# Rotary queries and keys of a decoder layer: the PSUM copy on ScalarE, the shuffle from SBUF, the cosine product on GpSimd

## What is computed

```python
qkv = layernorm(x) @ w_atten.T
q, k, v = split(qkv, 3)                      # 16 heads of 32 features
x0, x1 = even, odd features of q (and of k)
rotated = [x0 * cos - x1 * sin, x1 * cos + x0 * sin]
att = softmax(causal(rotated_q @ rotated_k.T / sqrt(32)))
x = x + (att @ v) @ w_proj.T
x = x + cross_attention(layernorm(x), ctx)
x = x + moe(layernorm(x))
```

## Time and profile before

| | |
|---|---|
| median of 3 runs | 1183.74 us (1178.89 to 1186.48) |
| profiled execution | 1181.09 us, its span 1179.3 us |
| PE busy | 1069.3 us, 91% |
| DVE busy | 600.1 us, 51% |
| ACT busy | 490.7 us, 42% |
| POOL busy | 177.7 us, 15% |

### The profile page before, as it was taken

How to read it: one execution, slowest core, us unless ns; L and a number is a source line. 1 busy time by engine, 2 the same in 40 slices (tenths; PEclk the granted TensorE clock), 3 DMA queues, 4 the chain that set the end, 5 groups by cost and what they waited for, 6 DMA issues and landing times.

```text
span 1179.3 us, 18650 instructions
## 1 busy us (share of the span) xinstructions
PE 1069.3 (91%) x6128; PEld 762.2 (65%) x6128; DVE 600.1 (51%) x1592; ACT 490.7 (42%) x1269; POOL 177.7 (15%) x204
## 2 busy tenths in 40 slices
PE   5778899799988898998988899998999999999998
PEld 2344444445544455445464678987889888889997
DVE  3456626656546666365464545563443344443565
ACT  1246634446615556345475432313443344342221
POOL 2121102211101112021100000011211111111232
PEclk9879999799999899998999999998999999999999
DMA  5934503213503335033160301135244444422554
GB/s 180 223 55 60 66 17 54 43 25 62 89 2 54 55 54 108 1 54 54 22 160 1 110 27 63 36 112 205 90 149 158 145 145 145 153 82 89 169 163 152
DMA packets 55524, 107.14 MB, mean 91 GB/s; under 512 B 5584, under 2 KB 16336, under 8 KB 55440
## 3 DMA queue, kind: packets, MB, share of 16 engines
q1 hardware_dynamic: 49840, 87.72, 31.5%
q0 software_dynamic: 5600, 18.35, 5.5%
HBM read 59.66 MB, written 21.23 MB: 69 GB/s over the span
## 4 chain that ended last, share of the span: by engine, by line
PE 73%; DVE 13%; issue 5%; DMA 4%; ACT 4%; POOL 1%; DVEq 0%; SPq 0%; ACTq 0%; POOLq 0%
PE ps L1005 19%; PE ps L812 10%; PE ps L1015 10%; PE ps L835 5%; PE ps L863 5%; PE ps L904 4%; PE ps L854 4%; PE ps L926 3%; PE ps L824 2%; PE ps L995 2%; DMA ks<-rope_b 2%; DVE gu_lo L1277 2%; DVE probs L1161 2%; DMA routed_x<-xn_d,table_cur 2%; PE ps L1023 1%
## 5 line engine op out<-in xcount | busy, mean ns | idle before, releaser
L1161 DVE CUSTOM_DVE_ANT_0 probs<-ps,mask 128x128 f32<-128x128 f32 (+3 forms) x256 | 123.8, 489 | 189.1 <-PE ps L824 129.4
L631 ACT COPY probsT<-ps 128x128 f32<-128x128 f32 (+3 forms) x256 | 109.3, 427 | 186.6 <-PE ps L835 185.5
L824 PE MATMUL ps<-ks,qs 96*128 96x256 f32 (+2 forms) x256 | 143.0, 562 | 26.5 <-DVE mx L1161 19.9
L623 ACT ACTIVATE probs<-probs,nb 128x128 f32<-128x128 f32 (+3 forms) x256 | 145.9, 570 | 49.3 <-DVE nb L1166 48.7
L812 PE MATMUL ps<-xnT,wa_sb 128*128 128x512 f32 x256 | 126.7, 620 | 16.0 <-DVEq L1147 15.2
L835 PE MATMUL ps<-ident,probs 128*128 128x128 f32 x640 | 125.0, 297 | 0.3
L1416 DVE TENSOR_TENSOR hidden<-sg,ps 128x352 f32<-128x352 f32 x69 | 35.9, 520 | 151.5 <-ACT sg L719 151.5
L835 PEld LDWEIGHTS ps<-ident,probs 128*128 128x128 f32 x640 | 81.2, 149 | 45.7 <-issue 39.2
L719 ACT ACTIVATE sg<-ps 128x352 f32<-128x352 f32 x69 | 32.0, 464 | 182.9 <-PE ps L1005 179.6
L824 PEld LDWEIGHTS ps<-ks,qs 96*128 96x128 f32 x256 | 52.3, 204 | 63.4 <-issue 35.7
L1015 PE MATMUL ps<-d_hi,h_hi 128*128 128x512 f32 (+1 forms) x207 | 89.9, 434 | 1.3 <-DVE h_lo L1420 1.3
(11 more groups left out here) (155 smaller groups left out, 1988.8 us busy)
## 6 DMA issues: line engine op xcount, KB each, us to landing
gu_raw<-in_we SPq DMA_DIRECT2D x10, 1408.0 KB
y_d<-y_sb SPq DMA_DIRECT2D x37, 256.0 KB
qs<-rope_b SPq DMA_DIRECT2D x32, 256.0 KB, 5.0
ks<-rope_b SPq DMA_DIRECT2D x32, 256.0 KB, 6.2
shared_x<-xn_d SPq DMA_DIRECT2D x32, 256.0 KB
d_raw<-in_we SPq DMA_DIRECT2D x10, 512.0 KB
qs<-rope_a SPq DMA_DIRECT2D x16, 256.0 KB, 7.0
ks<-rope_a SPq DMA_DIRECT2D x16, 256.0 KB, 6.6
```

The lines of the kernel that those rows point to most:

```text
L623: nc.scalar.activation(pr, pr, ACT.Exp, bias=nb[:, n % 2, h:h + 1], scale=SCALE, accum_out=sums[:, n % 2, h:h + 1]).then_inc(exp_done, 1)
L631: nc.scalar.copy(probsT[n % 2][:, h, 0:w], ps[:, T_BANK + h % 2, 0:w]).then_inc(pT_done, 1)
L824: nc.tensor.matmul(ps[:, S_BANK + h % 2, 0:w], qs[:, g % 2, h, i * P:(i + 1) * P], ks[:, g % 2, h, 0:w], start=True, stop=True).then_inc(s ...
L1161: nc.vector.tensor_tensor_reduce(probs[n % TT][:, h, 0:w], ps[:, S_BANK + h % 2, 0:w], mask[:, TOKENS - w:], 1.0, LOWEST, ALU.add, ALU.max ...
```

## The change

ACT copies the raw queries or keys from `QK_BANK` to `rope_b` (`copy_raw`), right behind its `probsT` copy of the same place, or behind the exponentials where there is none, and the end of this copy releases the bank (`rope_copied` replaces `qk_used`). DVE's shuffle reads this copy in SBUF. The cosine product goes to GpSimd, in place on `rope_b` and behind the sine product. DVE's add waits for both products. The add, the rounding copy, the subtraction, the tables of places and the DMAs stay.

```diff
--- before.py
+++ after.py
@@ -295,9 +295,10 @@
         v_mm = sem("v_mm")
         v_done = sem("v_done")
         qk_mm = sem("qk_mm")
-        qk_used = sem("qk_used")
         rope_link = sem("rope_link")
+        rope_copied = sem("rope_copied")
         rope_sine = sem("rope_sine")
+        rope_cosine = sem("rope_cosine")
         rope_done = sem("rope_done")
         stacked = sem("stacked")
         s_mm = sem("s_mm")
@@ -362,7 +363,7 @@
         W_LOADS = 7
         STACK = 2 * 3 * 16
         ROUTER_LINKS = 19
-        ROPE_LINKS = 4
+        ROPE_LINKS = 3
 
         def weight_chunks(gu, d):
 
@@ -530,7 +531,8 @@
                     low, high = rope_a[i], rope_b[i]
                     pool.wait_ge(rope_link, e * ROPE_LINKS + 1)
                     nc.gpsimd.tensor_tensor(low[:], low[:], sin_sb[:], ALU.mult).then_inc(rope_sine, 1)
-                    pool.wait_ge(rope_link, e * ROPE_LINKS + 4)
+                    nc.gpsimd.tensor_tensor(high[:], high[:], cos_sb[:], ALU.mult).then_inc(rope_cosine, 1)
+                    pool.wait_ge(rope_link, e * ROPE_LINKS + 3)
                     nc.gpsimd.tensor_tensor(low[:].bitcast(F32R), low[:], high[:], ALU.subtract).then_inc(rope_done, 1)
 
             def beside(b, last=False):
@@ -637,6 +639,14 @@
                 act.wait_ge(inverse_mm, b * STEPS + n + 1)
                 nc.scalar.copy(yT[:, g, i * P:(i + 1) * P], ps[:, T_BANK, INVERSE_COLS[i]])\
                     .then_inc(inverse_done, 1)
+
+            def copy_raw(b, g, i):
+
+                e = 2 * g + i
+                if not isinstance(b, int) or b or g:
+                    act.wait_ge(stacked, b * (GROUPS * STACK) + g * STACK)
+                act.wait_ge(qk_mm, b * (2 * GROUPS) + e + 1)
+                nc.scalar.copy(rope_b[i][:], ps[:, QK_BANK, :]).then_inc(rope_copied, 1)
 
             def cross(p, ln2, ln3, place):
 
@@ -684,6 +694,9 @@
                             for n in turned_inverses(r):
                                 copy_inverse(b, n)
                         place = GH * r + h
+                        for b_raw, g, i, steps in queries_keys(place, b, last, ROPE_PLACES):
+                            if 0 in steps:
+                                copy_raw(b_raw, g, i)
                         if p is not None:
                             copy_values(b, place)
                         if p is not None:
@@ -698,6 +711,8 @@
                             high_part(0, 0, SPLIT_PLACES.index(place))
 
             copy_turned(xnT, 0, range(TT))
+            for i in range(2):
+                copy_raw(0, 0, i)
             attend(0, None)
             act.wait_ge(w_loaded, 16 * W_LOADS)
             with act.Fori(1, BATCHES - 1) as b:
@@ -797,7 +812,7 @@
                 ln = next_ln(b)
                 pe.wait_ge(ln_xn, ln * TT + t + 1)
                 if t == 0:
-                    pe.wait_ge(qk_used, b * (2 * GROUPS) + 2 * GROUPS)
+                    pe.wait_ge(rope_copied, b * (2 * GROUPS) + 2 * GROUPS)
                 else:
                     pe.wait_ge(ln_xnT, ln * TT + t)
                 turn_tile(ln, t, xn1, NEXT_BANK)
@@ -806,7 +821,7 @@
 
                 e = 2 * g + i
                 if chunks[0] == 0 and (not isinstance(b, int) or b or e):
-                    pe.wait_ge(qk_used, b * (2 * GROUPS) + e)
+                    pe.wait_ge(rope_copied, b * (2 * GROUPS) + e)
                 for c in chunks:
                     col = i * DIM + g * P
                     last = nc.tensor.matmul(ps[:, QK_BANK, :], wa_sb[:, c, col:col + P], xnT[:, c, :],
@@ -1135,20 +1150,18 @@
 
                 e = 2 * g + i
                 links = b * (2 * GROUPS * ROPE_LINKS) + e * ROPE_LINKS
-                raw, low, high = ps[:, QK_BANK, :], rope_a[i], rope_b[i]
+                low, high = rope_a[i], rope_b[i]
                 if 0 in steps:
                     if not isinstance(b, int) or b or g:
                         dve.wait_ge(stacked, b * (GROUPS * STACK) + g * STACK)
-                    dve.wait_ge(qk_mm, b * (2 * GROUPS) + e + 1)
+                    dve.wait_ge(rope_copied, b * (2 * GROUPS) + e + 1)
                     pass_wait(dve)
-                    nc.vector.stream_shuffle(low[:], raw, swap).then_inc(rope_link, 1)
-                    nc.vector.tensor_tensor(high[:], raw, cos_sb[:], ALU.mult).then_inc(rope_link, 1)
-                    dve.wait_ge(rope_link, links + 2)
-                    dve.nop().then_inc(qk_used, 1)
+                    nc.vector.stream_shuffle(low[:], high[:], swap).then_inc(rope_link, 1)
                 if 1 in steps:
                     dve.wait_ge(rope_sine, b * (2 * GROUPS) + (e + 1))
+                    dve.wait_ge(rope_cosine, b * (2 * GROUPS) + (e + 1))
                     nc.vector.tensor_tensor(low[:], low[:], high[:], ALU.add).then_inc(rope_link, 1)
-                    dve.wait_ge(rope_link, links + 3)
+                    dve.wait_ge(rope_link, links + 2)
                     nc.vector.tensor_copy(high[:].bitcast(F32R), low[:]).then_inc(rope_link, 1)
 
             def mask_and_max(b, n, h):
```

## The result

The changed kernel takes 1209.8 us in the median of 4 runs (1209.6 to 1215.8), beside 1185.1 for the kernel before in 4 runs: a ratio of 1.0227, 95% interval 1.0184 to 1.0271. It is slower clear of noise; whether by more than 2% is not decided. The forecast was 1184 with a range up to 1196. The profiled execution of the changed kernel is the slowest of its five, 1215.8 us (mean granted clock 0.931); the other four lie at 1209.6 to 1210.2 with clocks of 0.935 to 0.938. So what follows explains 34.7 us of span (1214.0 against 1179.3) where the median shows 25.

The account below looks back on a forecast made before the run. The prediction took TensorE (PE), busy 91% of the span, as the bound, so only its waits counted. Terms of -8.5, +9.8 and +1.5 us made +2.8 on 1181.1, 1183.9, forecast as 1184, range 1174 to 1196.

Parts of the forecast that it names:

- What bounds the kernel: TensorE (PE), busy 91% of the span, so changes on other engines can pay only through a wait of PE.
- Term 1: Queries (i=0) inside attention: the raw bank is released sooner, shortening twelve of PE's 13 waits for it; -8.5 us.
- Term 2: Keys (i=1) inside attention: ACT's late copy delays shuffle and add, PE waits on mask steps in eleven pairs; +9.8 us.
- The pair in batch 0: Second late keys pair of batch 0: the add 2.16 us late, all of it landing on PE.
- the worst of batches 1 and 2: Late keys pair with the add 2.09 us late and 1.0 of room at place 8's mask step: 1.1 lost.
- One pair that was to keep its time: Keys for group 1 of batch 0: ACT is found waiting there, so no loss was expected.
- Term 3: First query and key pair, alone at the start with nothing hiding the longer chain; +1.5 us, all on PE.
- The third: Rival: late keys win, the early release only moves PE to its next wait on DVE; 1192.4 to 1198, chance 0.18.
- the signs that were named: Bank waits 15.2 to about 6 us, mask waits 19.9 up by about 8; busy DVE -21, ACT +19, GpSimd +41.
- The fourth: Rival, the port: GpSimd holds DVE's `nb` step 0.65 us in eleven late pairs, delaying the exponentials; 1191, chance 0.12.
- What the trace didn't show: Durations assumed without a row: shuffle from SBUF 0.73 us, two GpSimd products without a wait between at least 1.27 each.

Follow-up runs that it names:

- d1: The changed kernel, but VectorE shuffles from PSUM at its old time and ScalarE's copy for GpSimd's cosine product follows that shuffle; 1183.0 us, ratio 0.9985.
- q1: The changed kernel with the change for the queries alone, the keys on the path of before; 1190.4 us, four executions from 1174.0 to 1196.7.
- k1: The changed kernel with the change for the keys alone, the queries on the path of before; 1216.9 us, ratio 1.0255.
- w2: The kernel before, with PE repeating its transposes of place 9 of each group (192 more over the kernel); 1199.3 us, ratio 1.0125.
- l1: The changed kernel with the keys' add, cast and subtraction two places later (place 9 instead of 7); 1193.6 us, ratio 1.0064.
- c1: The changed kernel with the cosine product back on VectorE, made from the SBUF copy behind its shuffle; 1190.1 us, ratio 1.0054.

## Why the prediction was wrong

**What bounds the kernel: the step that failed.** "A change on the other engines can only pay through a wait of PE" is true of PE's start times and false of its speed. The sum priced each wait at its own length and took PE's 1069 us of busy time as fixed. It is not: 34.6 us of busy time came with the same matmuls. Two rival readings, a sum of waits that was wrong and GpSimd's hold on DVE, are out by the 0.2 us of idle time and by d1. The row of the clock was on the page that I read first, 0.7 in one slice of batch 0 and one of batch 1, and no term, rival or bound of the range had it. By the account, one us at half clock costs 0.40 us, and the changed kernel has 85.9 us more of it.

The Trainium skill, "TensorE: Matmul & The Clock Gate", section HAM oscillation — how this bites in real kernels, tells of a kernel in which a wait for a DMA ahead of each short stretch of matmuls throttles PE's clock, so that the stretch begins at half speed. The waits there are about 3 to 5 us. The traces agree that low stretches follow waits, but not on the size: the ones of 20.5 and 17.1 us came with waits of 0.82 and 0.84 us, while 4.6 us of waiting at place 10 brought d1 no more low time there than the kernel before has. So the page gives a reason to look at the clock, and no forecast of this loss.

**Term 1** (-8.5 us): right in size as a sum of waits, though no kernel got it as time. One place measured 0.86 against 0.87, the bank waits fell by 10.1 us to 5.1 ("about 6"), and q1's idle time fell by 4.7 although its first pair's wait for the stacking DMA rose to 3.3 us from 0.5.

**Term 2** (+9.8 us): right as a wait. The pair in batch 0 measured 2.32 us against 2.16, the worst of batches 1 and 2 1.2 against 1.1; mask waits rose by 10.7 ("about 8"), k1's idle time by 8.1. The three pairs of batch 0 cost 0.5, 2.3 and 2.1 us at their mask steps where the forecast had 0.97, 2.16 and 1.88. One pair that was to keep its time didn't: for group 1 of batch 0 the add came 3.65 us behind the shuffle instead of 2.93, and PE's longest wait went from 2.7 to 4.9 us, 1.2 net of shorter waits just before it. What was missed is what such waits start.

**Term 3** (+1.5 us): looks more than twice as large, and isn't. PE's first scores came at 42.85 instead of 39.01:

```profile
32.04 1.27 POOL L536 TENSOR_TENSOR rope_a<-rope_a,rope_b 128x512 fp32r<-128x512 f32 x1 [1.34 <-DVE rope_b L1165]
```

```profile
42.85 0.39 PE L839 MATMUL ps<-ks,qs 96*128 96x256 f32 x1 [3.26 <-DMA ks<-rope_b]
```

against 28.35 and 39.01 in the earlier trace rows. But the clock rose at 19.65 us there and at 15.46 before, during the first projection. In w2, whose start is that of the kernel before, it rose at 20.50 and the first scores came at 41.31; in l1, whose start is that of the changed kernel, it rose at 14.47 and they came at 40.75. Like with like, the change costs 42.85 - 41.31 = 1.5 us or 40.75 - 39.01 = 1.7 us, and the time of the first rise, which differs between runs of one start, 2.1 to 2.3.

**The rivals.** The third named the right side and the right culprit, the late keys, with 1192 to 1198; the time went 12 us past its end, since it too was made of waits. Of the signs that were named, the waits, ACT's and GpSimd's time all came about as written; only DVE's time didn't, and none of them looked at PE's own busy time. The fourth's open question is settled: the tile `nb` in the changed kernel, answering its fixed 0.17 us before,

```profile
L1179 DVE TENSOR_SCALAR nb<-mx x64: 169/170/1169, 50.3 to 656.7; 128x4 f32<-128x4 f32 x64
```

is held by GpSimd for up to 1.17 us (the one at 233.77 ended with the sine product that ran from 233.65 to 234.92), but ACT's waits for it went from 48.7 to 47.8 us, and d1 has the same at no cost. The Trainium skill's rule ("SBUF — State Buffer", Who interferes with whom) holds for this small step too.

**What the trace didn't show.** The shuffle from SBUF takes 0.73 us, as assumed, and two GpSimd products 1.27 each:

```profile
L1159 DVE STREAM_SHUFFLE rope_a<-rope_b x32: 721/730/737, 22.3 to 614.2; 128x512 f32<-128x512 f32 x32
...
L534 POOL TENSOR_TENSOR rope_b<-rope_b,cos_sb x32: 1262/1271/1279, 24.4 to 616.2; 128x512 f32<-128x512 f32 x32
```

DVE waited 21.8 us for ACT in 13 shuffles (9.6 of it once, at the start) and 17.1 us for GpSimd in 11 adds (at most 3.3).

## What to carry to other kernels

Where PE is the bound, a wait has two prices: its length, and the clock. Sum both: read the clock row by stage first, and give the range a bound for the stretches at half clock that the kernel already shows. Don't take a trade of waits in one place for waits in another as free because the sum is equal. Test a suspected clock loss by putting spare matmuls into the wait: if the kernel gets faster with more work and its low time falls, it was the clock. And work moved from DVE to GpSimd doesn't free DVE by its own length: here 21.6 us were saved and 24.8 came back as held steps.

## What was new about the hardware

- With unchanged idle time (106.3 and 106.5 us), the time at 1.2 GHz nearly doubled (87.3 and 169.0 us). From within a wait of 0.82 us on, the clock stayed low for 20.5 us in which PE was busy for 19.2.
- The same start has its first rise of the clock at about 15 us in some runs and about 20 in others, worth 2 us; q1's four runs spread over 22.7 us with clocks of 0.962 to 0.947.
- In c1 the cosine product on DVE has two SBUF inputs and runs beside GpSimd's sine. The tile view of the sine, against a median of 1.27 us before and after:

```profile
L533 POOL TENSOR_TENSOR rope_a<-rope_a,sin_sb x32: 1699/1776/1784, 21.0 to 592.5; 128x512 f32<-128x512 f32 x32
```

GpSimd gives way by 0.5 us to a DVE product of 0.69 us that had begun first. In the kernel before the same product read PSUM and SBUF, and the sine kept its 1.27.
